# Fourth layer 17 steps behind the third, its x-sums in one step, and one semaphore for the scan

## The reference

```python
# layer 0: a weight made from cond (LayerNorm, gelu MLP, rank-8 factors), applied to every token
x = x + (x + einsum('btc,bco->bto', x, base + einsum('bdr,bkr->bdk', x_a, x_b)))
# layer 1
x = x + tanh(einsum('bsi,hi->bsh', x, W_ih) + (hx @ W_hh.T + b_hh + b_ih)[:, None, :])
# layers 2 and 3: an LSTM each, over 2048 steps in sequence, h0 = cond, c0 = 0
def step(carry, xp_t):                     # xp_t = x_t @ Wx + b
    prev_h, prev_c = carry
    a = xp_t + prev_h @ Wh                 # (2, 2048): gates i, f, o, g of 512 each
    next_c = sigmoid(f) * prev_c + sigmoid(i) * tanh(g)
    next_h = sigmoid(o) * tanh(next_c)
    return (next_h, next_c), next_h
x = x + lstm(x, Wx2, Wh2, b2)
x = x + lstm(x, Wx3, Wh3, b3)
```

## Time and profile before

| | us |
|---|---|
| median of 3 runs | 11900.89 |
| lowest, highest | 11898.32, 11901.08 |
| the profiled execution | 11900.05 |
| its span on the core | 11898.2 |
| mean granted clock of TensorE, share of full speed | 0.999 |

### The profile page before, as it was taken

One profiled execution on the slowest core, in us unless ns is written; L12 is line 12 of the kernel. 1 busy time (PEld: TensorE's weight loads), 2 busy tenths in 40 slices (PEclk: granted clock), 3 DMA queues, 4 the chain that ended last, 5 costly groups with the idle time before them and its releaser, 6 DMA issues.

```text
span 11898.2 us, 435945 instructions
## 1 busy us (share of the span) xinstructions
PE 11828.7 (99%) x231604; PEld 2698.0 (23%) x100532; DVE 8509.1 (72%) x46342; ACT 3758.9 (32%) x24698; POOL 1418.6 (12%) x5238
## 2 busy tenths in 40 slices
PE   8999999999999999999999999999999999999999
PEld 5222222222222222222222222222222222222222
DVE  2677777777777777777777777777777777777776
ACT  2233333333333333333333333333333333333332
POOL 4011111111111111111111111111111111111110
PEclk9999999999999999999999999999999999999999
DMA  4000000000000000000000000000000000000000
GB/s 164 25 4 5 4 5 4 5 5 4 5 5 4 5 5 4 5 4 5 4 5 5 4 5 5 4 5 5 4 5 4 5 4 5 5 4 5 5 5 3
DMA packets 374546, 107.86 MB, mean 9 GB/s; under 512 B 349594, under 2 KB 357830, under 8 KB 372436
## 3 DMA queue, kind: packets, MB, share of 16 engines
q1 hardware_dynamic: 362372, 61.96, 2.8%
q0 software_dynamic: 3504, 11.56, 0.3%
q10 hardware_dynamic: 6560, 6.32, 0.2%
HBM read 62.98 MB, written 16.78 MB: 7 GB/s over the span
## 4 chain that ended last, share of the span: by engine, by line
PE 99%; DVE 0%; issue 0%; ACT 0%; POOLq 0%; POOL 0%; DVEq 0%
PE bank L80 89%; PE bank L874 7%; PE bank L518 1%; PE bank L531 1%; PE bank L484 0%; DVE gates_t L1055 0%; DVE gates_t L1062 0%; ACT gate_o L950 0%; DVE state L1085 0%; DVE state L1088 0%; DVE state L1081 0%; ACT tanh_c L952 0%; DVE pre L1068 0%; DVE pre L1061 0%; DVE g_fc L1065 0%
## 5 line engine op out<-in xcount | busy, mean ns | idle before, releaser
L80 PE MATMUL bank<-wh,state 128*6 128x512 bf16 x196608 | 11055.6, 379 | 20.8 <-DVE state L1088 20.8
L1054 DVE STREAM_TRANSPOSE gates_t<-bank 128x256 f32<-128x256 f32 x4096 | 1843.6, 450 | 2015.3 <-PE bank L80 2013.7
L80 PEld LDWEIGHTS bank<-wh,state 128*6 128x6 bf16 x65536 | 1568.1, 86 | 7400.5 <-issue 6498.0
L945 ACT ACTIVATE gate_if<-pre 128x8 f32<-128x8 f32 x4096 | 859.8, 210 | 7256.0 <-DVE pre L1059 7256.0
L1081 DVE TENSOR_TENSOR state<-gate_o,tanh_c 128x8 f32<-128x8 f32 x4096 | 688.2, 168 | 836.0 <-ACT tanh_c L952 811.2
L1062 DVE STREAM_TRANSPOSE gates_t<-bank 128x128 f32<-128x128 f32 x4096 | 1252.5, 306 | 0.0
L1055 DVE STREAM_TRANSPOSE gates_t<-bank 128x128 f32<-128x128 f32 x4096 | 1122.9, 274 | 0.0
L983 POOL TENSOR_TENSOR y<-x,state 128x8 f32<-128x8 f32 x2048 | 434.5, 212 | 5374.2 <-DVE state L1088 5374.2
L950 ACT ACTIVATE gate_o<-pre 128x8 f32<-128x8 f32 x4096 | 855.0, 209 | 642.8 <-DVE pre L1068 642.4
L983 POOL TENSOR_TENSOR x<-x1r,state 128x8 f32<-128x8 f32 x2048 | 434.5, 212 | 4961.2 <-DVE state L1088 4961.2
L952 ACT ACTIVATE tanh_c<-g_c 128x8 f32<-128x8 f32 x4096 | 854.7, 209 | 9.7 <-DVE g_c L1072 9.7
(11 more groups left out here) (124 smaller groups left out, 3490.6 us busy)
## 6 DMA issues: line engine op xcount, KB each, us to landing
w<-in_w SPq DMA_DIRECT2D x8, 2048.0 KB, 13.2
out<-y_rows SPq DMA_DIRECT2D x1020, 8.0 KB, 1.8
wx<-in_x SPq DMA_DIRECT2D x16, 512.0 KB, 5.4
x1p<-x_t_all SPq DMA_DIRECT2D x128, 64.0 KB, 2.6
x1r<-x_t_all SPq DMA_DIRECT2D x128, 64.0 KB, 2.6
x_t_all<-wx ACTq DMA_DIRECT2D x6, 1024.0 KB, 4.8
wx<-in_Wh POOLq DMA_DIRECT2D x8, 512.0 KB, 4.2
wx<-in_Wh POOLq DMA_DIRECT2D x16, 256.0 KB, 4.9
```

The costliest lines, as they stand in the source:

```text
L80: return pe.add_instruction(mybir.InstMatmult(name=nc.get_next_instruction_name(), engine=mybir.EngineType.PE, ins=[pe.lower_ap(moving), p ...
L945: act.activation(gate_if[l][:, 1, :, 1], pre[l][:, HB:2 * HB], ACT.Sigmoid).then_inc(S[l]["f"], 1)
L1054: dve.transpose(gates_t[l][:, 0:gf, NS * NB:], banked[:, 0:gf]).then_inc(s["trans_if"], 1)
```

## The change

`SUMS` for L3 goes from eight x-sums in each of steps 0 and 1 to all sixteen in step 0; by `beside`, eight stand behind L2's block and eight behind L3's. L2's x-sums start a step earlier, with two in step 1. `LAG` goes from 19 to 17, so that there are 17 steps of one layer at either end and 2,031 of both; L3's first time step of a chunk is in step 1, where it was in step 3. `ROWS_AT` follows, from 4 to 2. In the chunks 1 and 128 step 0 has one layer only; there all four quarters are turned in the same step, and POOL adds their bias ahead of the residual.

The semaphores `fc` and `g`, for both of which the scan waited, become one, `terms`, raised by one each; the scan waits for twice the count. So that DVE keeps one count n for all of its waits, the other semaphores for which it waits are raised by 2 (`BOTH`), and their other waiters' numbers follow.

```diff
-SUMS = ((0, 0, 2, 2) + (1,) * 12, (8, 8) + (0,) * 14)
-
-LAG = CH + 2 + 1
+SUMS = ((0, 2) + (1,) * 14, (16,) + (0,) * 15)
+
+LAG = CH + 1
...
+BOTH = 2
...
-    def count(self, l, s):
-
-        return self.v * (BODY * CH) + (self.i * CH - LAG * l + s + 1)
+    def count(self, l, s, each=1):
+
+        return self.v * (BODY * CH * each) + (self.i * CH - LAG * l + s + 1) * each
...
-        return [x[:3] for x in found if x[3] == NH - 1]
+        found = [x[:3] for x in found if x[3] == NH - 1]
+        if self.number in (1, NCH) and s < 2:
+
+            own = [(L3, -1, q) for q in range(4)]
+            found = [x for x in found if x not in own] + (own if s == 0 else [])
+        return found
+
+    def own_turned(self, s):
+
+        return self.number in (1, NCH) and s == 0
...
-                            matmuls(l).then_inc(S[l]["mm"], 1)
+                            matmuls(l).then_inc(S[l]["mm"], BOTH)
...
-                            act.activation(g_fc[l][:, :, 0], pre[l][:, 2 * HB:3 * HB], ACT.Tanh).then_inc(S[l]["g"], 1)
+                            act.activation(g_fc[l][:, :, 0], pre[l][:, 2 * HB:3 * HB], ACT.Tanh).then_inc(S[l]["terms"], 1)
...
-                            residual(l, t, s)
-                            for x in t.done_before(l, s):
-                                add_bias(x[0], t, *x[1:])
+                            if t.own_turned(s):
+                                for x in t.done_before(l, s):
+                                    add_bias(x[0], t, *x[1:])
+                                residual(l, t, s)
+                            else:
+                                residual(l, t, s)
+                                for x in t.done_before(l, s):
+                                    add_bias(x[0], t, *x[1:])
...
-                            n = t.count(l, step)
+                            n = t.count(l, step, BOTH)
...
                             dve.tensor_tensor(g_fc[l][:, :, 1], gate_if[l][:, 1, :, 1], g_c[l][:, :, 1],
-                                              ALU.mult).then_inc(s["fc"], 1)
+                                              ALU.mult).then_inc(s["terms"], 1)
...
-                            dve.wait_ge(s["fc"], n)
-                            dve.wait_ge(s["g"], n)
+                            dve.wait_ge(s["terms"], n)
```

More of the change, by code:

```diff
@@ L810, in emit @@
                     if t.load_r:
-                        sp.wait_ge(S[L2]["res"], t.count(L2, 0))
+                        sp.wait_ge(S[L2]["res"], t.count(L2, 0, BOTH))
                         load_x1(sp, x1r, t.slot(1), t.at(1), s_x1r)
@@ L864, in project @@
                         if q == 0 and l == L3:
-                            pe.wait_ge(S[L2]["res"], t.at(d + 1) * CH + 1)
+                            pe.wait_ge(S[L2]["res"], t.at(d + 1) * (CH * BOTH) + BOTH)
                         if t.reused(d, q):
@@ L951, in emit @@
                             act.wait_ge(S[l]["c"], n)
-                            act.activation(tanh_c[l][:, :], g_c[l][:, :, 1], ACT.Tanh).then_inc(S[l]["tanh"], 1)
+                            act.activation(tanh_c[l][:, :], g_c[l][:, :, 1], ACT.Tanh).then_inc(S[l]["tanh"], BOTH)
                         if t.number == 0:
@@ L984, in residual @@
                                        part(state[l], 0).rearrange("p h (b o) -> p h b o", o=1),
-                                       ALU.add).then_inc(S[l]["res"], 1)
+                                       ALU.add).then_inc(S[l]["res"], BOTH)
                 def add_bias(l, t, d, q):
@@ L1028, in turn_rows @@
                     i = t.slot(d)
-                    dve.wait_ge(S[L3]["res"], t.at(d + 1) * CH + 1)
+                    dve.wait_ge(S[L3]["res"], t.at(d + 1) * (CH * BOTH) + BOTH)
                     dve.wait_ge(s_out[i], (t.half(d) + 1) * OUT)
@@ L1053, in emit @@
                             dve.wait_ge(s["mm"], n)
-                            dve.transpose(gates_t[l][:, 0:gf, NS * NB:], banked[:, 0:gf]).then_inc(s["trans_if"], 1)
-                            dve.transpose(gates_t[l][:, gf:ifg, NS * NB:], banked[:, gf:ifg]).then_inc(s["trans_g"], 1)
+                            dve.transpose(gates_t[l][:, 0:gf, NS * NB:], banked[:, 0:gf]).then_inc(s["trans_if"], BOTH)
+                            dve.transpose(gates_t[l][:, gf:ifg, NS * NB:], banked[:, gf:ifg]).then_inc(s["trans_g"], BOTH)
                             dve.wait_ge(s["trans_if"], n)
@@ L1061, in emit @@
                             dve.tensor_reduce(sums[:, gf:ifg], terms[:, gf:ifg], AXX, ALU.add).then_inc(s["pre_g"], 1)
-                            dve.transpose(gates_t[l][:, ifg:, NS * NB:], banked[:, ifg:]).then_inc(s["trans_o"], 1)
+                            dve.transpose(gates_t[l][:, ifg:, NS * NB:], banked[:, ifg:]).then_inc(s["trans_o"], BOTH)
                             dve.wait_ge(s["f"], n)
                             dve.tensor_tensor(g_fc[l][:, :, 1], gate_if[l][:, 1, :, 1], g_c[l][:, :, 1],
-                                              ALU.mult).then_inc(s["fc"], 1)
+                                              ALU.mult).then_inc(s["terms"], 1)
                             dve.wait_ge(s["trans_o"], n)
                             dve.tensor_reduce(sums[:, ifg:], terms[:, ifg:], AXX, ALU.add).then_inc(s["pre_o"], 1)
-                            dve.wait_ge(s["fc"], n)
-                            dve.wait_ge(s["g"], n)
+                            dve.wait_ge(s["terms"], n)
                             dve.tensor_tensor_scan(g_c[l][:, :, :].rearrange("p n two -> p (n two)"),
@@ L1082, in emit @@
                                               tanh_c[l][:, :].rearrange("p (h b) -> p h b", h=NH),
-                                              ALU.mult).then_inc(s["h"], 1)
+                                              ALU.mult).then_inc(s["h"], BOTH)
                             dve.wait_ge(s["h"], n)
                             dve.tensor_tensor(part(st, 1), part(st, 0), upper(part(st, 0)),
-                                              ALU.subtract).then_inc(s["r1"], 1)
+                                              ALU.subtract).then_inc(s["r1"], BOTH)
                             dve.wait_ge(s["r1"], n)
```

10 lines of the change are left out of this document (5 added, 5 removed).

## The result

The changed kernel takes 12407.37 us (median of 5, 12403.59 to 12410.62), the kernel before 11900.58 us beside it: a ratio of 1.0426 (95% interval 1.0411 to 1.0441), 506.8 us more. I had forecast 12135 us in a range up to 12200. The sign and the new wait were right; more than half of the loss came from a part that I had costed at nothing.

A forecast was written before the change was run, and what follows sets the result against it. PE was taken to bound the kernel, with about 0.2 us of chain slack per step. 11900.05 + 243.2 (new wait) - 0.9 (merge) - 7.8 (less lag) = 12134.6, forecast 12135 us, range 12112 to 12200.

The forecast's parts named there:

- the new wait: After L3's step-0 block, PE waits for DVE to turn q0 before writing q2: 1.93 us, 126 times, +243.2 us.
- At no cost: Moved x-sums, output-row turns, POOL biases, SP loads and stores, and semaphores raised by two: claimed to add nothing.
- the part before: Merged semaphore at the scan: saves 0.05 us, counted in the new wait and 18 single-layer steps, -0.9 us there.
- signs of a wrong forecast: In the profile after: gap between L3's block and q2 under 1.8 or over 2.0 us, or a second PE wait.
- The pairs: Middle steps of both layers: 5.40 us with one x-sum, about 0.2 us chain slack; a shorter chain gains 0.
- The second wait: L3's chunk starting one step after its last sum: next block ready at 5.70, due 5.84; cover 0.14 us, cost 0.
- The rival: Late bias of q3 delays L3's chunk by 0.2 to 0.5 us uncovered: +25 to +63 us; chance 12%.
- The first wait: PE idle between L3's step-0 block and q2 until q0 is turned: 1.93 us, bounds 1.80 to 1.98.
- The ends: Single-layer steps at start and end: -0.9 us from the merge and -7.8 us from two steps less of lag.
- the rival of 10%: PE's clock falls after every second new wait, 63 x 1.65 = +104 us, 12239 us; chance 10%.
- Not slower: Rival: q0 turned before L3's block ends, so PE keeps its pace: 11892 us, -0.07%; chance 3%.

The follow-up runs named there:

- the old order alone: Changed kernel with the x-sum order and LAG 19 of before, keeping the merged semaphore and raises by two: 12039.55 us, ratio 1.0117.
- the kernel with only the merge: Changed kernel, only the scan's merged semaphore waited for at twice the count, all others raised by one: 12139.46 us, ratio 1.0202.
- four banks: Changed kernel with a PSUM bank of its own for each of L3's four quarters: 12137.79 us, ratio 1.0200.
- The trace with ones: Changed kernel with all semaphores raised by one and the scan waiting for f*c and tanh(g) apart: 12171.54 us, ratio 1.0229.

## Why the prediction was wrong

- **The step that failed** is under "At no cost": "Raising a semaphore by two for one is the same instruction." It is not, where the instruction that raises also waits. Five waits of the chain became instructions of their own, 0.06 to 0.07 us each, some 0.32 us together and 0.26 us net of the merge. I had priced just such a wait, 0.06 us, in the part before, as the scan's second one, and didn't ask what else would get one. From this follow the errors in the pairs, in the second wait and at the ends. Two of my own signs of a wrong forecast came true: the gap behind L3's block is over 2.0 us, and PE has a second kind of wait.
- **The pairs.** I took the chain's slack (2.81 - 2.55 us, less 0.05 us to PE, so 0.2 us) as given, with a shorter chain. It became 0.26 us longer, 5.45 us a loop against 5.40 us of PE's work, and the bound moved from PE to the chain in the steps with one x-sum: 149 us over the 30 other places of the changed kernel, 139 us with the old order alone (twelve such steps a chunk for fourteen).
- **The second wait.** I had its mechanism, its place and its cover of 0.14 us, and put 12% on up to 63 us. In the changed kernel (all engines, L2's step 1 and L3's step 1):

```profile
6017.54 2.77 PE L80 MATMUL bank<-wh,state 128*6 128x512 bf16 x48
...
6022.77 0.17 DVE L1103 TENSOR_TENSOR state<-state 128x8 f32<-128x8 f32 x1
...
6023.25 0.88 POOL L1003 TENSOR_TENSOR area<-turned,bias_all 128x128 f32<-128x128 f32 x2
...
6024.22 0.22 ACT L952 COPY gates_t<-area 128x32 f32<-128x32 f32 x1 [2.01 <-POOL area L1003]
...
6024.55 0.22 DVE L1075 TENSOR_REDUCE pre<-gates_t 128x16 f32<-128x64 f32 x1 [0.67 <-ACT gates_t L952]
...
6026.37 0.17 DVE L1103 TENSOR_TENSOR state<-state 128x8 f32<-128x8 f32 x1
```

L2's block ends at 6017.54 + 2.59 = 6020.13. The state is whole at 6022.77 + 0.17, +2.81 (2.51 by the forecast's figures, 0.22 + 2.34 - 0.05), POOL's bias of q3 ends at +4.00 (3.65), the reduce starts at +4.42 (3.93), L3's state is whole at +6.41 and its block starts at +6.46 (5.70), due at 5.84. Eleven hand-overs on this way have a separate wait that they lacked before: five in L2's step, POOL's residual, ScalarE's copy and four in L3's step; at 0.06 to 0.07 us each they make up about 0.7 of the 0.76 us by which the block comes later. With the waits in their instructions the forecast 0 was right to 0.03 us. The rival named the right wait and missed its size: 0.71 us, 88 us.
- **The first wait** was right: 1.93 us forecast, 1.94 us in the kernel with only the merge, 2.13 us in the changed one (median 2.06), where two of the slower hand-overs lie in it; four banks took off 126 x 2.14.
- **The ends**: -8.7 us forecast. With ones and the merge they are 9.2 us shorter in the profiled execution (238.8 us in all, of which 245.6 in the chunks 2 to 126 and 2.4 in chunk 127), so this term was right; in the changed kernel only 0.8 us, since its single steps take 5.45 us.
- **The clock**: the rival of 10% had it that every second wait is followed by a fall. Five of the 126 were. The mean of the middle hides it; short stretches of 3.4 us from 1978.2, 5732.9, 8176.8, 8740.0 and 9490.9 us show it. The middle and the last of them (us, busy, clock, DMA share, GB/s), then PE's timeline there:

```profile
2000.00:11000.00 9000.00, 8747.28 (x171800) 1.00 0.03 4
9490.90:9494.40 3.50, 3.47 (x68) 0.51 0.02 5
```

```profile
9490.93 3.60 PE L885 MATMUL bank<-wx,x 128*32 128x128 f32 x64 [2.14 <-DVE turned L1039]
9494.34 2.77 PE L80 MATMUL bank<-wh,state 128*6 128x512 bf16 x48
```

The eight x-sums behind that wait take 3.41 us (9490.93 to 9494.34), where they take 1.75 us at the upper level, 2.4 GHz; the granted clock was 0.50, the 1.2 GHz level. All five falls stand behind a first wait of 1.98 to 2.21 us by the view's count, where most are 1.85 us; three others as long had none. At my 1.65 us a fall they cost 8 us of the 507. The trace with ones has two falls in the middle, the trace with only the merge, whose waits are 1.72 us by this count, has none. The rule of the Trainium skill weighed ahead (TensorE: Matmul & The Clock Gate, "HAM oscillation — how this bites in real kernels"), by which a wait in every iteration brings the engine back to half clock each time, is drawn there from waits of some 3 to 5 us behind some 2 us of matmuls. Taken for all 126 waits of 2 us here, each behind some 90 us of matmuls, as I did ahead, it gives far too much: five falls, not 126.
- **Not slower**: fell, as expected.

## What to carry to other kernels

When semaphores are merged, or their counts scaled so that several waits can share a register, count the instructions of the trace or of the built program before and after: a wait that no longer fits into its instruction costs 0.07 us here, and in a recurrence each one can lie on the path. Compute the loop time of a dependent chain (5.19 us) beside the work of the bounding engine (5.40 us) and see how few such prices lie between them. Look at the distribution over the steps as well as at the median: the rare late hand-overs came on top. The same holds for the clock, whose mean over a long stretch hid five falls. Where a producer fills two buffers, and the consumer empties them only behind other work that itself waits for the producer, the producer stalls as soon as it must fill a third buffer at once. Two more buffers removed that wait here, and in the kernel before other work of the producer stood between.

## What the runs showed of the hardware

- A wait in an instruction of its own adds 0.06 to 0.07 us to a hand-over (0.27 us for 0.20 us from h to its remainder), whether it is there for a raise by two or for a second semaphore. A raise by two adds nothing where the wait stays in its instruction (0.20 us from the first to the second remainder in both kernels).
- Some hand-overs are 0.2 to 0.36 us late, at the same places of the loop's code in all three passes. From h to its remainder there are none in the kernel before, 32 with a separate wait for h, and 73 of 4,096 with the old order and raises by two; the cause is open.
- Of 126 idle times of PE of about 2 us, one each 94 us, five were followed by 3.4 us at a granted clock of 0.50, the 1.2 GHz level; behind the others it stayed at 2.4 GHz.
